# Where the weight conversions of the next-but-one expert stand in an expert's first tile

## The reference

```
x = x + layernorm(attention(layernorm(x)))     # linear attention: elu(q)+1, elu(k)+1
x = x + layernorm(moe(layernorm(x)))
# moe: 32 experts, each token goes to 8 of them
h = silu(xs @ w1[e]) * (xs @ v1[e])            # 512 -> 192
out[token] += (h @ w2[e]) * weight             # 192 -> 512
```

## Time and profile before

| | us |
|---|---|
| median of 3 runs (lowest to highest) | 2731.66 (2720.08 to 2733.62) |
| the profiled execution's own time | 2733.02 |
| its span, first to last instruction | 2731.3 |
| TensorE matmuls busy | 2348.3 (86%) |
| VectorE busy | 1465.7 (54%) |
| ScalarE busy | 1259.8 (46%) |
| GpSimd busy | 944.5 (35%) |

### The profile page before, as it was taken

The page is one execution under the profiler, slowest core; times in us unless marked ns, Lnnn a source line. Parts: engine busy times, 40 slices in busy tenths (PEclk is TensorE's granted clock), DMA queues, the critical chain, the costliest instruction groups (busy, mean ns, idle before and its releaser), DMA issues.

```text
span 2731.3 us, 64310 instructions
## 1 busy us (share of the span) xinstructions
PE 2348.3 (86%) x12196; PEld 2007.1 (73%) x12197; DVE 1465.7 (54%) x4712; ACT 1259.8 (46%) x2706; POOL 944.5 (35%) x1015
## 2 busy tenths in 40 slices
PE   7998999999899999738897888788997888988990
PEld 6886688888688888627786777677786777877880
DVE  4555567777677777534453444444444434444446
ACT  3344556666565666424343333443443434444443
POOL 1211034544345545523332333223332323323332
PEclk9999999999999999859998999899999999989995
DMA  3333213323333233356766667776767676777767
GB/s 117 100 112 81 66 65 118 126 108 136 120 111 128 105 117 126 130 177 139 174 130 171 145 132 165 178 167 136 161 121 188 132 184 115 164 162 171 131 131 273
DMA packets 173370, 376.49 MB, mean 138 GB/s; under 512 B 21088, under 2 KB 21088, under 8 KB 173152
## 3 DMA queue, kind: packets, MB, share of 16 engines
q0 software_dynamic: 62816, 148.93, 27.7%
q1 hardware_dynamic: 110464, 226.65, 26.0%
HBM read 182.68 MB, written 192.83 MB: 137 GB/s over the span
## 4 chain that ended last, share of the span: by engine, by line
DMA 19%; issue 12%; PE 10%; SPq 9%; DVEq 3%; DVE 3%; ACT 1%; ACTq 0%; POOL 0%; another core or an unknown queue 0%; POOLq 0%
DMA BIG<-sorted_rows 16%; DMA moe_sum<-X,aidx 2%; PE bank L415 2%; PE bank L416 2%; PE bank L417 2%; PE bank L406 2%; SPq L317 2%; SPq L301 1%; SPq L306 1%; SPq L341 1%; DVEq L650 1%; SPq L307 1%; DVEq L640 1%; ACT BIG L542 1%; SPq L342 1%
## 5 line engine op out<-in xcount | busy, mean ns | idle before, releaser
L1365 POOL DMA_INDIRECT moe_sum<-X,aidx x292 | 460.7, 1578 | 1025.2 <-issue 578.5
L866 PE MATMUL bank<-WB,XH 128*128 128x512 f32 x1536 | 478.3, 393 | 0.0
L415 PE MATMUL bank<-WB,XL 128*128 x1168 | 441.0, 378 | 23.8 <-DVE XL L642 23.2
L416 PE MATMUL bank<-WB,XH 128*128 x1168 | 411.6, 352 | 0.0
L417 PE MATMUL bank<-WB,XH 128*128 x1168 | 411.0, 352 | 0.0
L406 PE MATMUL bank<-ident,BIG 128*128 128x128 f32 x1168 | 195.5, 293 | 189.5 <-DMA BIG<-sorted_rows 183.3
L406 PEld LDWEIGHTS bank<-ident,BIG 128*128 128x128 f32 x1168 | 137.4, 147 | 270.7 <-DMA BIG<-sorted_rows 248.1
L866 PEld LDWEIGHTS bank<-WB,XH 128*128 128x128 f32 x1536 | 290.6, 189 | 60.4 <-issue 0.5
L866 PE MATMUL bank<-WB,XL 128*128 128x512 f32 x768 | 316.6, 412 | 10.2 <-DVE XL L1170 10.2
L866 PE MATMUL bank<-WB,SH 128*128 128x512 f32 x1024 | 318.9, 393 | 0.0
L650 DVE SCALAR_TENSOR_TENSOR BIG<-BIG,bank x292 | 101.2, 347 | 392.9 <-ACT BIG L481 203.8
(11 more groups left out here) (179 smaller groups left out, 4428.9 us busy)
## 6 DMA issues: line engine op xcount, KB each, us to landing
BIG<-sorted_rows SPq DMA_DIRECT2D x293, 274.0 KB
sorted_rows<-BIG SPq DMA_DIRECT2D x65, 274.0 KB
X<-x_in SPq DMA_DIRECT2D x64, 256.0 KB, 2.7
RAW<-w_in SPq DMA_DIRECT2D x16, 768.0 KB
LATE<-w_in SPq DMA_DIRECT2D x16, 768.0 KB
moe_sum<-LATE SPq DMA_DIRECT2D x34, 256.0 KB, 2.9
LATE<-x_in SPq DMA_DIRECT2D x32, 256.0 KB
RAW<-wo_in SPq DMA_DIRECT2D x16, 512.0 KB, 3.5
```

The lines of the kernel that those rows point to most:

```text
L415: nc.tensor.matmul(eu[s][:, 0:UP], XL[:, s, k, :], wh, start=k == 0, stop=False)
L416: nc.tensor.matmul(eu[s][:, 0:UP], XH[:, s, k, :], wh, start=False, stop=False)
L866: last = nc.tensor.matmul(ps, w, m, start=start and i == 0, stop=stop and i == len(terms) - 1)
L1365: nc.gpsimd.indirect_dma_start(acc_dram[:, :], bass.IndirectOffsetOnAxis(aidx[:, s:s + 1], 0), rows, None, compute_op=ALU.add).then_inc(s_ ...
```

## The change

In an expert's first tile, ScalarE's six weight pieces stood between the tile's own four operations: one behind `rows_high`, one behind `silu`, two behind `act_high`, two behind `evacuate`. Now all six stand behind `evacuate`. On VectorE one stood behind `rows_low`, one behind `gate`, and four behind `add_index`; now all six stand behind `add_index`. The pieces themselves, their number, sizes and waits are as they were, and so are all other engines' programs.

```diff
 # ScalarE
                     rows_high(g + 1, other)
-                    if split:
-                        weights_high(e + 2, (q + 2) % WSETS, q % 2, 0)
                     silu(g, same)
-                    if split:
-                        weights_high(e + 2, (q + 2) % WSETS, q % 2, 1)
                     act_high(g - 1, other)
-                    if split:
-                        weights_high(e + 2, (q + 2) % WSETS, q % 2, 2)
-                        weights_high(e + 2, (q + 2) % WSETS, q % 2, 3)
                     evacuate(g - 2, same)
                     if split:
-                        weights_high(e + 2, (q + 2) % WSETS, q % 2, 4)
-                        weights_high(e + 2, (q + 2) % WSETS, q % 2, 5)
+                        for piece in range(len(PIECES)):
+                            weights_high(e + 2, (q + 2) % WSETS, q % 2, piece)
 # VectorE
                     rows_low(g + 1, other)
-                    if split:
-                        weights_low(e + 2, (q + 2) % WSETS, q % 2, 0)
                     gate(g, same, e)
-                    if split:
-                        weights_low(e + 2, (q + 2) % WSETS, q % 2, 1)
                     act_low(g - 1, other)
                     add_index(g - 2, same)
                     if split:
-                        for piece in range(2, len(PIECES)):
+                        for piece in range(len(PIECES)):
                             weights_low(e + 2, (q + 2) % WSETS, q % 2, piece)
```

## The result

| | before | changed |
|---|---|---|
| median of 20 runs (lowest to highest), us | 2731.98 (2720.08 to 2738.95) | 2738.41 (2728.80 to 2752.64) |
| ratio, with 95% interval | | 1.0028 (1.0015 to 1.0041) |
| profiled execution, its own time, us | 2733.02 | 2736.08 |
| VectorE busy, us | 1465.7 | 1468.0 |

The kernel became slower by 6.4 us between the medians, 0.28% by the ratio; the forecast was 2737.5. This is within the 0.5% that was called no change, but both intervals leave out 1.

The account below looks back on a forecast made before the run. VectorE's block at an expert's first tile was taken to hold both row loads and TensorE. Terms 3.8+1.0+0.9 = 5.7 us gave 2738.7 by the profiled execution's clock, 2737.3 as median, rounded to 2737.5; range 2723 to 2750.

Parts of the forecast that it names:

- The gap ahead of gate: VectorE, from the rows' low half to gate: without a piece between, 0.89 us from start to start, 0.20 of it idle.
- ScalarE's piece 0 and VectorE meet at the same moment: At the boundary shown, ScalarE's piece 0 is there at 1499.26 and VectorE is ready for it at 1499.28.
- The sum at a direct boundary: Where the row-tail copy directly follows the last piece and the load follows it: copy 0.32 us later, twelve boundaries 3.8 us.
- TensorE's wait there: TensorE's wait for VectorE's subtraction (the rows' low half) at such a boundary: 0.8 us instead of 0.49.
- VectorE's stalls ahead of the copy: Code stalls marked "issue" ahead of the row-tail copy: the prediction is wrong if their number or length changes.
- The very first boundary: Piece 0 loses its cover in the wait for silu, 0.47 us, and waits for ScalarE's evacuation, 0.5: 1.0 us.
- The six late boundaries: VectorE comes late, ScalarE is far ahead: 0.29 us uncovered each, TensorE has 0.5 to spare; 0 to 1.7, taken 0.9 us.
- The 11 others: Boundaries where the copy waits for something later or SyncE is busy with a new expert's transfers: no cost, at most 3.5 us.
- `rows_high` of first+2 ends 0.6 us ahead of the subtraction, so it costs nothing: ScalarE's next tile: behind six pieces it is done at 1502.06, the subtraction needing it comes at 1502.69 at the earliest.
- Gaps empty: Rival: VectorE waits through both old gaps because ScalarE's piece 0 comes later; 17.7 us slower, 2749; chance 0.15.
- Hidden anyway: Rival: the row load could not start much earlier and later waits absorb 0.3 us; no change, 2731.7; chance 0.17.
- The tile's own work earlier pays: Rival: `act_low`, index and evacuation come earlier, GpSimd's add could leave 0.65 us sooner; 19.5 us faster, 2712; chance 0.08.

Follow-up runs that it names:

- Experiment 3: The changed kernel with piece 0 back in its old place on ScalarE and VectorE, pieces 1 to 5 as in the change; 1.0013 of the kernel before.
- Experiment 1: The kernel before with only VectorE's six pieces moved behind `add_index`, ScalarE's order as before; 1.0035 of the kernel before, 2728.07 against 2716.08 us.
- The rotated kernel with extra work: Kernel before, next tile's row conversion ending each ScalarE and VectorE pass, plus an unread VectorE subtraction behind it at boundaries; 1.0037, without the subtraction 0.9993.
- experiment 2: The kernel before with only ScalarE's six pieces moved behind `evacuate`, VectorE's order as before; 1.0082 of the kernel before, 2742.25 against 2716.08 us.
- The rotated kernels: Kernel before with tile g+2's row conversion ending ScalarE's and VectorE's pass g; rows ahead of VectorE's last four, ScalarE's last two pieces 0.9895, ahead of all six 0.9927.

## Why the prediction was right, and where it was not

*The gap ahead of gate.* Right: forecast 0.89 us from the low half to gate with 0.20 idle, measured 0.92 with 0.22. Experiment 3 removes it by putting one piece back.

*ScalarE's piece 0 and VectorE meet at the same moment.* Right. Forecast 1499.26 and 1499.28, that is 3.2 us behind `rows_high`; measured 3.23 (1503.50-1500.27). Experiment 1, with ScalarE far ahead, has VectorE's piece 0 at the same place behind L642, 1.84 us in both.

*The sum at a direct boundary.* Forecast 0.32 us, measured 0.33 in the boundary shown (5.14 against 4.81) and 0.37 in the medians of the twelve (table). The sum took piece 0 at 1499.32, where its own terms give 1499.28, so they carry 0.28 and the last 0.04 has no source. TensorE's wait there was forecast at 0.8 us and was 1.04. ScalarE's second `rows_high` was forecast 5.4 us behind the first and came at 5.38. VectorE's stalls ahead of the copy (idle time with the mark "issue"), whose change would have spoiled the comparison, were 76.7 us in 31 places before and 76.9 in 32 after.

*The very first boundary.* Off: I took 1.0 us. VectorE's timeline of the changed kernel there:

```profile
1212.10 0.69 DVE L635 TENSOR_TENSOR XL<-bank,XH  x1 [0.31 <-ACT XH L476]
1215.85 0.35 DVE L643 SCALAR_TENSOR_TENSOR BIG<-BIG,bank  x1 [3.06 <-ACT BIG L481]
...
1220.23 0.18 DVE L633 COPY BIG<-BIG  x1
```

From gate to the copy it is 4.38 us against 3.76 (1216.82 to 1220.58 in the trace of before, whose gate is in the earlier trace rows), 0.62 more. But gate itself came 3.75 us behind the low half, where before it came 4.29, and the net is 0.1. silu was ready sooner because TensorE's up ran at the higher of its two clock levels earlier. These are the stretches 1213.5 to 1215.0, of before and of changed; the number ahead of the DMA share is the granted clock:

```profile
1213.50:1215.00 1.50, 1.50 (x6) 1.50 (x6) 0.18 (x1) 0.00 (x0) 0.00 (x0) 0.50 0.01 3
1213.50:1215.00 1.50, 1.50 (x10) 1.38 (x9) 0.00 (x0) 0.34 (x2) 0.00 (x0) 0.98 0.00 0
```

In these 1.5 us TensorE had 6 matmuls under way at 0.50 (1.2 GHz), and 10 at 0.98 (nearly 2.4 GHz). Ahead of the tiles it had stood idle for 19.8 us, until 1207, in both. The moment of the rise isn't an effect of the change alone: in the repeat of the changed kernel the clock stood at 0.84 from 1208 to 1209 and at 1.00 from there on. Here it made up for most of the 0.62.

*The six late boundaries.* The block grew by 0.3 us there as well: 1629.32 to 1634.44 is 5.12. TensorE's next up stood at 1635.53, 6.21 us behind the low half, and before 1631.38-1625.17 = 6.21 (the low half's start is from the trace of before; up is in the earlier trace rows). So TensorE's slack took it up in this one, as the lower bound said. The block grew by 0.31 or 0.32 us at all six; what they cost together isn't shown.

*The 11 others.* That they cost nothing isn't shown. At the boundary of 2227 us, where the copy follows the last piece at once but the next load belongs to a new expert, the block grew from 4.81 to 5.15 us, and TensorE's next up came 0.35 us later behind the low half (6.07 against 5.72). The time from one boundary to the next differs by up to 5 us between the two profiled executions of the changed kernel, so the traces can't say which boundaries carry the 6.4 us.

*What the sum left out.* The step "`rows_high` of first+2 ends 0.6 us ahead of the subtraction, so it costs nothing" was right about the subtraction and left out the queue. VectorE's queue prepares an operation while the engine works on the one before, but it holds still at the wait for ScalarE's last piece: at all 12 direct boundaries it goes on 0.05 us after that piece has ended. That was 4.3 to 4.7 us behind the first `rows_high` before, and is 5.3 to 5.7 us now. So the preparation of the next pass has less of VectorE's pieces to hide behind. VectorE's timeline at the boundary at 1684 us of before, first before, then changed:

```profile
1690.49 0.69 DVE L642 TENSOR_TENSOR XL<-bank,XH  x1
1691.09 0.34 DVE L650 SCALAR_TENSOR_TENSOR BIG<-BIG,bank  x1
```

```profile
1694.80 0.69 DVE L635 TENSOR_TENSOR XL<-bank,XH  x1
1695.91 0.35 DVE L643 SCALAR_TENSOR_TENSOR BIG<-BIG,bank  x1 [0.43 <-issue]
```

0.60 against 1.11 us. This is not so everywhere. The idle time ahead of that gate is new, 0.40 to 0.43 us, at 5 of the 12 direct boundaries, is 0.02 or nothing at 6, and grew from 0.55 to 1.30 at the one of 2480 us. The five are those at which the queue stands still for another 0.46 to 0.49 us behind the preparation of the subtraction, in both kernels; why it does so only there isn't shown. The chain of the changed kernel in order of time, at 1694 us, where gate's first wait (L640) passed at 1695.05 by the trace, and then at 1506 us, where the queue goes straight on:

```profile
1694.48 0.09 DVEq L635
...
1695.12 0.04 DVEq L641
```

```profile
1506.57 0.09 DVEq L635
1506.75 0.02 DVEq L640
```

Over the direct boundaries gate of first+1 is 0.73 us later (table), not 0.32, and the add of tile first-1 leaves 9.86 instead of 9.00 us behind `rows_high` (medians). The rotated kernel with extra work shows that such a delay can cost time even when the copy stands still. But experiment 1 speaks against a large share of it in the 6.4 us: there gate+1 came only 0.45 us later, the new idle time was absent at those five, and the ratio was 1.0035 all the same. The intervals are 0.17% to either side, too wide to tell the share from nothing. So that the total of 5.7 us comes so near the 6.4 measured is partly luck: the first boundary's 1.0 measured 0.1 net in these two executions, the late ones' 0.9 and the zero of the 11 others are not measured, and the delay of gate+1 was missing. How the 6.4 us divide is open.

*The rivals.* "Gaps empty" would be 17.7 us: outside the interval (4 to 11 us); it nearly happened in experiment 2, where piece 0 was really waited for. "Hidden anyway" is outside both intervals. "The tile's own work earlier pays" did come true as far as its first half: at the boundary shown the index was 0.62 us earlier, and GpSimd's add of tile first-2 left 4.59 us behind `rows_high` (1504.86-1500.27) instead of 5.21. But the add of first-1 left 9.41 us behind it, instead of 8.96, and nothing was gained.

GpSimd's timeline of the changed kernel (compare rows 14):

```profile
1504.86 1.56 POOL L1354 DMA_INDIRECT moe_sum<-X,aidx  x1 [2.76 <-DMA moe_sum<-X,aidx]
1509.68 1.55 POOL L1354 DMA_INDIRECT moe_sum<-X,aidx  x1 [3.25 <-DMA moe_sum<-X,aidx]
```

The Trainium skill's advice to interleave where the most-contended engine changes (Perfetto Trace Analysis, Optimization Strategy) is borne out in sign by the change, 0.28%, though no run shows that the most-contended engine changes here. The rotated kernels add that where the pieces stand matters more: with pieces 0 and 1 still in between but the row-tail copy taken out from behind the other four, the kernel gained 1.05%, and with all six in one block behind the copy it still gained 0.73%.

## What to carry to other kernels

Deferrable work can cover moments in which an engine's queue is still preparing the next operation, and it should not be stacked ahead of an operation that another queue waits for. Here the second counted for more. Before moving such work, ask which small instruction behind it raises a semaphore for a transfer, here a copy of 0.18 us, and put that one ahead. And don't move the producer's pieces behind the point where the consumer needs them: moved alone on ScalarE they cost 0.82%, moved alone on VectorE 0.35%, no more than both together.

## What the runs showed of the hardware that I had not expected

VectorE's register and address preparation for one gate operation is worth 0.3 us of engine time when nothing runs ahead of it (0.92 us from start to start, where 0.60 is possible). A wait that ends late further up in the queue, here that for ScalarE's last piece, can make it visible behind the next pass's subtraction (1.11 us). An extra subtraction of 0.7 us with a wait for its own end moved the gate of the next pass by 1.48 us, of which some 0.3 are such preparation between the subtraction and the gate (0.90 us from start to start at ten of the twelve boundaries instead of 0.60).
